# Attention's output divided in the layout of its sum and carried as rows by DMA to the gate's product

## The reference

```
src  = layernorm(x)
q, k, v = src @ q_w, src @ k_w, src @ v_w       # 16 heads of 16
s    = q k^T / 4 * (2 * sigmoid(sum(q * scale_w)))
out  = softmax(s) @ v                            # (2, 2048, 256)
gate = sigmoid(out @ gate_w + gate_b)
xr   = layernorm(src + (out * gate) @ out_w) * n1_g + n1_b
# router: top 2 of 8 experts from xr @ moe_gate_w, the one of larger index is applied,
# then two more layernorms and a residual
```

## Time and profile before

| | us |
|---|---|
| median of the runs | 2483.32 |
| the profiled execution | 2487.67 |
| its span, first to last instruction | 2487.7 |
| busy in the span: TensorE, VectorE, ScalarE, GpSimd | 2369.6, 2102.9, 1796.4, 992.7 |
| attention's units: first and last copy of `pv` to `pvs` start at | 822.5 and 2139.6 |
| first instructions of the gate's stage | 2143.5 |

### The profile page before, as it was taken

The page is one execution under the profiler, slowest core; times in us unless marked ns, Lnnn a source line. Parts: engine busy times, 40 slices in busy tenths (PEclk is TensorE's granted clock), DMA queues, the critical chain, the costliest instruction groups (busy, mean ns, idle before and its releaser), DMA issues. The chain is left out here.

```text
span 2487.7 us, 45337 instructions
## 1 busy us (share of the span) xinstructions
PE 2369.6 (95%) x16331; PEld 1028.3 (41%) x16331; DVE 2102.9 (85%) x4156; ACT 1796.4 (72%) x2368; POOL 992.7 (40%) x1186
## 2 busy tenths in 40 slices
PE   7899999999689999999999999999999999996996
PEld 5566655655443223223222222223223222473663
DVE  6778788989689999999998999898899996283886
ACT  4888887777334887878787787787787878762664
POOL 1687878888741222211221221221211011255664
PEclk8999999999889999999999999999999999997998
DMA  3322233223240220304012030040040000125892
GB/s 110 112 88 90 85 92 105 89 99 96 67 137 14 37 43 7 59 14 65 14 31 35 14 59 7 14 65 2 14 65 2 2 2 24 52 83 204 297 304 101
DMA packets 105956, 174.09 MB, mean 70 GB/s; under 512 B 21218, under 2 KB 80658, under 8 KB 100596
## 3 DMA queue, kind: packets, MB, share of 16 engines
q1 hardware_dynamic: 98996, 156.08, 23.6%
q0 software_dynamic: 6016, 14.49, 1.7%
q10 hardware_dynamic: 720, 0.62, 0.1%
HBM read 145.21 MB, written 27.02 MB: 69 GB/s over the span
## 5 line engine op out<-in xcount | busy, mean ns | idle before, releaser
L1682 DVE TENSOR_REDUCE max_part<-round_psum 128x1 f32<-128x512 f32 x2048 | 1269.0, 683 | 101.8 <-PE round_psum L1591 96.8
L1647 ACT ACTIVATE p_exp<-score_psum 128x1024 f32<-128x1024 f32 x1024 | 993.3, 1022 | 213.7 <-PE score_psum L1576 209.3
L1591 PE MATMUL round_psum<-k_stack,q_stack 64*128 64x512 bf16 x2048 | 705.5, 384 | 10.7 <-DVE max_part L1682 6.5
L1567 PE MATMUL score_psum<-q_stack,k_stack 64*128 64x512 bf16 x2048 | 599.0, 379 | 0.9 <-ACT p_exp L1647 0.2
L1576 PE MATMUL score_psum<-q_stack,k_stack 35*128 35x512 bf16 x2048 | 594.6, 378 | 0.0
L1622 PE MATMUL pv_psum<-p_exp,values 128*17 128x512 f32 x4096 | 539.6, 598 | 0.0
L1591 PEld LDWEIGHTS round_psum<-k_stack,q_stack 64*128 64x128 bf16 x2048 | 189.4, 93 | 600.3 <-DVE max_part L1682 510.7
L672 PE MATMUL rot<-tokens_t,w_in 128*128 128x512 f32 x576 | 271.7, 603 | 0.2
L1576 PEld LDWEIGHTS score_psum<-q_stack,k_stack 35*128 35x128 bf16 x2048 | 188.9, 94 | 116.0 <-issue 0.5
L1729 POOL TENSOR_TENSOR rden<-pv_out,minus_one 128x16 f32<-128x16 f32 x31 | 90.0, 2903 | 332.4 <-ACT pv_out L1665 330.1
L1715 POOL CAST max_parts<-max_neg 128x16 bf16<-128x16 f32 x96 | 20.4, 212 | 365.8 <-DVE max_neg L1688 343.4
(11 more groups left out here) (300 smaller groups left out, 3472.9 us busy)
## 6 DMA issues: line engine op xcount, KB each, us to landing
cum_rows_in<-cum_rows SPq DMA_DIRECT2D x64, 512.0 KB, 3.8
expert_w<-in_expert_w SPq DMA_DIRECT2D x24, 1028.0 KB
tokens_t<-in_expert_w SPq DMA_DIRECT2D x15, 1028.0 KB
cum_pairs_in<-cum_rows SPq DMA_DIRECT2D x240, 64.0 KB, 2.8
qk_rows<-qk_parts SPq DMA_DIRECT2D x64, 192.0 KB, 3.1
q_stack<-qk_rows SPq DMA_DIRECT2D x84, 128.0 KB, 8.1
k_stack<-qk_rows SPq DMA_DIRECT2D x84, 128.0 KB, 9.1
token_rows<-tokens SPq DMA_DIRECT2D x12, 512.0 KB, 3.7
```

Source lines behind the costliest of these rows:

```text
L1567: nc.tensor.matmul(ebank[i // 2][:, i % 2, :], ks[rows, n % 2, plane, k * P:(k + 1) * P], qs[rows, n % 2, plane, q * BLK:(q + 1) * BLK], s ...
L1591: nc.tensor.matmul(bank[step][:, :], qs[rows, n % 2, plane, at:at + P], ks[rows, n % 2, plane, keys * BLK:(keys + 1) * BLK], start=True, s ...
L1647: nc.scalar.activation(pt[:, (k * 2 + pair) % 4, :, :], ebank[pair][:, :, :], ACT.Exp).then_inc(*exped.up(u, k, pair))
L1682: nc.vector.tensor_reduce(mx[:, c * HG + h, keys:keys + 1], bank[step][:, :], AX_X, ALU.max).then_inc(*maxed.up(u, k, i))
```

## The change

`turn_out` and `turn` go. A unit's output stays in `pvs` with channels as rows and is divided there; that needs the denominators, one row per head, as inverses on each of the head's 16 rows. Five items, `OUT_AT`, take the place of `turn_out`: in step 2 of the next unit `out_low`: SP stores the four denominator rows to DRAM; step 3 `out_column`: SP loads them as a 128x16 tile; step 6 `out_inverse`: GpSimd's power, and SP stores the result; step 8 `out_spread`: SP loads each head's row of inverses to its 16 partitions (into `rspread`, the place of the value weights); step 11 `out_rows`: GpSimd multiplies 128x512, and SP copies each head's 16 rows by DMA to where `gate` reads them. ScalarE's next copy of `pv` waits for these copies instead of the division. The last unit spreads its denominators by four matmuls with a broadcast column of the identity, and VectorE takes the reciprocal and multiplies. `oT` is now a view of the tensor `tokens` itself, with the rows of all eight blocks. In the gate's stage `turn` is gone from the lists of TensorE and ScalarE, `xr` of a block is written over the block's rows in `oT`, and its store is two transfers. The lists and the `busy` counts are otherwise the same. The code behind SP's loop is unchanged.

```diff
+OUT_AT = (2, "out_low"), (3, "out_column"), (6, "out_inverse"), (8, "out_spread"), (11, "out_rows")
...
-        plan(u * KT + KT + 2, ("turn_out", u, 0, 0))
+        for wait, what in OUT_AT:
+            plan(u * KT + KT + wait, (what, u, 0, 0))
...
-    for t in range(-LEAD, total + 4):
+    for t in range(-LEAD, total + OUT_AT[-1][0] + 1):
...
+    rspread = S.w_v.rearrange("p k d -> p (k d)")
+    den_dram = nc.dram_tensor("denominators", (2, HG, BLK), F32, kind="Internal").ap()
+    inv_dram = nc.dram_tensor("denominator_inverses", (2, HG, BLK), F32, kind="Internal").ap()
+    oT = attn[:, :, :].rearrange("p c d -> p (c d)").rearrange("p (k t) -> p k t", k=KD)
...
-    users = [step for step in order if step[0] in ("max", "turn_rows", "turn_out", *splits)]
+    users = [step for step in order if step[0] in ("max", "turn_rows", *splits)]
...
+                if what == "out_low" and u < NU - 1:
+                    sp_.wait_ge(*pv_out.at(u))
+                    for h in range(HG):
+                        low = h * 32 + HD
+                        nc.sync.dma_start(den_dram[u % 2, h:h + 1, :],
+                                          pvs[low:low + 1, :]).then_inc(*den_saved.up(u, h))
+                if what == "out_column" and u < NU - 1:
+                    sp_.wait_ge(*den_saved.at(u, HG - 1))
+                    if u:
+                        sp_.wait_ge(*inv_saved.at(u - 1))
+                    nc.sync.dma_start(rden[:, :], den_dram[u % 2].rearrange("h (a w) -> (h a) w", w=CPB * HG)
+                                      ).then_inc(*den_load.up(u))
+                if what == "out_inverse" and u < NU - 1:
+                    sp_.wait_ge(*inverse.at(u))
+                    nc.sync.dma_start(inv_dram[u % 2].rearrange("h (a w) -> (h a) w", w=CPB * HG),
+                                      rden[:, :]).then_inc(*inv_saved.up(u))
+                if what == "out_spread" and u < NU - 1:
+                    sp_.wait_ge(*inv_saved.at(u))
+                    if u:
+                        sp_.wait_ge(*divided.at(u - 1))
+                    for h in range(HG):
+                        nc.sync.dma_start(rspread[h * 32:h * 32 + HD, :], inv_dram[u % 2, h:h + 1, :].to_broadcast([HD, BLK])
+                                          ).then_inc(*spread.up(u, h))
+                if what == "out_rows":
+                    n, q = UNITS[u]
+                    b, g = GROUPS[n]
+                    if u == 0:
+                        sp_.wait_ge(*x1_saved.all())
+                    sp_.wait_ge(*(divided if u < NU - 1 else last_divided).at(u))
+                    for h in range(HG):
+                        row = (g % 2) * HG * HD + h * HD
+                        nc.sync.dma_start(oT[row:row + HD, g // 2, b * SEQ + q * BLK:b * SEQ + (q + 1) * BLK],
+                                          pvs[h * 32:h * 32 + HD, :]).then_inc(*out_saved.up(u, h))
...
-                if what == "turn_out":
+                if what == "out_low" and u == NU - 1:
                     pe.wait_ge(*pv_out.at(u))
-                    pe.wait_ge(*bank_read(before[step]))
-                    for c in range(CPB):
-                        t = nc.tensor.transpose(bank[step][:, c * P:(c + 1) * P], pvs[:, c * P:(c + 1) * P], K["ident"])
-                    t.then_inc(*out_turned.up(u))
+                    pe.wait_ge(*exped.at(u, KT - 1, 1))
+                    for h in range(HG):
+                        low = h * 32 + HD
+                        m = nc.tensor.matmul(ebank[0][h * 32:(h + 1) * 32, 0, :], K["ident"][:, low:low + 1].to_broadcast([P, 32]),
+                                             pvs[:, :], start=True, stop=True, skip_group_check=True)
+                    m.then_inc(*last_spread.up(u))
...
                     if u:
-                        act.wait_ge(*divided.at(u - 1))
+                        act.wait_ge(*out_saved.at(u - 1, HG - 1))
                     nc.scalar.copy(pvs[:, :], pv[:, :]).then_inc(*pv_out.up(u))
-                if what == "turn_out" and u < NU - 1:
-                    act.wait_ge(*out_turned.at(u))
-                    nc.scalar.copy(pvs[:, :], bank[step][:, :]).then_inc(*out_in.up(u))
...
-                    nc.vector.reciprocal(rden[:, :].unsqueeze(2), o[:, :, HD:HD + 1]).then_inc(*last_inverse.up(u))
+                    nc.vector.reciprocal(rspread, ebank[0][:, 0, :]).then_inc(*last_inverse.up(u))
                     ve.wait_ge(*last_inverse.at(u))
...
+                    nc.vector.tensor_tensor(pvs[:, :], pvs[:, :], rspread, ALU.mult).then_inc(*last_divided.up(u))
...
+                if what == "out_inverse" and u < NU - 1:
+                    if u == 0:
                         po.wait_ge(*one.at(0))
+                    po.wait_ge(*den_load.at(u))
+                    nc.gpsimd.tensor_tensor(rden[:, :], rden[:, :], minus[:, :].to_broadcast([P, CPB * HG]),
+                                            ALU.pow).then_inc(*inverse.up(u))
+                if what == "out_rows" and u < NU - 1:
+                    po.wait_ge(*spread.at(u, HG - 1))
+                    nc.gpsimd.tensor_tensor(pvs[:, :], pvs[:, :], rspread, ALU.mult).then_inc(*divided.up(u))
...
-                        if c == 0:
-                            pe.wait_ge(*heads_t.at(b, k))
-                        m = nc.tensor.matmul(gbank[c][:, :], w_gate[:, k, c * P:(c + 1) * P], oT[:, two, k, :],
+                        if (b, c, k) == (0, 0, 0):
+                            pe.wait_ge(*G.out_saved.at(NU - 2, HG - 1))
+                        if (b, c, k) == (NBLK - 1, 0, 0):
+                            pe.wait_ge(*G.out_saved.at(NU - 1, HG - 1))
+                        m = nc.tensor.matmul(gbank[c][:, :], w_gate[:, k, c * P:(c + 1) * P],
+                                             oT[:, k, b * BLK:(b + 1) * BLK],
```

More of the change, by code:

```diff
@@ L1503, in attention @@
     v_stored = sems.events("late_v_stored", late)
[L1504 to L1505 removed]
+    den_saved = sems.dma("denominator_save", [(u, h) for u in range(NU - 1) for h in range(HG)])
+    den_load = sems.dma("denominator_load", range(NU - 1))
+    inverse = sems.events("denominator_inverse", range(NU - 1))
+    inv_saved = sems.dma("inverse_save", range(NU - 1))
+    spread = sems.dma("inverse_spread", [(u, h) for u in range(NU - 1) for h in range(HG)])
     divided = sems.events("out_divided", range(NU - 1))
+    out_saved = G.out_saved
+    last_spread = sems.events("last_denominator_spread", [NU - 1])
     last_inverse = sems.events("last_denominator_inverse", [NU - 1])
[L1508 removed]
+    last_divided = sems.events("last_out_divided", [NU - 1])
     one = sems.events("minus_one_ready", [0])
@@ L1689, in _ @@
                                             negate=True).then_inc(*negated.up(u))
-                if what == "turn_out" and u == NU - 1:
-                    n, q = UNITS[u]
-                    b, g = GROUPS[n]
-                    o = bank[step][:, :].rearrange("p (n w) -> p n w", w=32)
-                    ve.wait_ge(*out_turned.at(u))
+                if what == "out_inverse" and u == NU - 1:
+                    ve.wait_ge(*last_spread.at(u))
                     ve.wait_ge(*divided.at(u - 1))
-                    nc.vector.reciprocal(rden[:, :].unsqueeze(2), o[:, :, HD:HD + 1]).then_inc(*last_inverse.up(u))
+                    nc.vector.reciprocal(rspread, ebank[0][:, 0, :]).then_inc(*last_inverse.up(u))
                     ve.wait_ge(*last_inverse.at(u))
-                    for c in range(CPB):
-                        nc.vector.tensor_tensor(heads(attn[:, b * KT + q * CPB + c, g * HG * HD:(g + 1) * HG * HD],
-                                                          HG, HD), o[:, c * HG:(c + 1) * HG, 0:HD],
-                                                    over_last(rden[:, c * HG:(c + 1) * HG], HD), ALU.mult)
+                    nc.vector.tensor_tensor(pvs[:, :], pvs[:, :], rspread, ALU.mult).then_inc(*last_divided.up(u))
         @block.gpsimd
@@ L1794, in __init__ @@
         self.x1_load = [sems.dma(f"x1_load{i}", range(i, NBLK, 3)) for i in range(3)]
+        self.out_saved = sems.dma("out_save", [(u, h) for u in range(NU) for h in range(HG)])
 BIAS_AT = [slice(first, first + 3 * NE) for first in (0, 32)]
@@ L1826, in gate_and_route, with xr_block, by_two, over_block @@
     iota = {n: iotas[:, at] for n, at in I_AT.items()}
-    oT = sb("attn_t", [P, 2, KD, BLK])
+    oT = attn[:, :, :].rearrange("p c d -> p (c d)").rearrange("p (k t) -> p k t", k=KD)
+    def xr_block(b):
+        return oT[:, :, b * BLK:(b + 1) * BLK].rearrange("p k (two d) -> p k two d", d=D)
+    def by_two(t):
+        return t.rearrange("p (k two) d -> p k two d", two=2)
+    def over_block(row):
+        return row.unsqueeze(1).unsqueeze(1).to_broadcast([P, KD, 2, D])
     sig = sb("gate_sig", [P, 2, BLK])
@@ L1863, in gate_and_route @@
     halves = [(b, i) for b in range(NBLK) for i in range(2)]
-    t_users = [(what, b) for what, b in order["PE"] if what in ("turn", "rows")]
```

(28 more changed lines are left out.)

27 lines of the change are left out of this document (3 added, 24 removed), and 8 rows, old and new, of the table STAGE5.

## The result

The changed kernel takes 2492.76 us (median of nine runs, 2490.18 to 2498.70), the kernel before 2486.91 us (nine runs beside it). The ratio is 1.0030 (95% interval 1.0019 to 1.0041). A second set of twelve runs gave 1.0019 (1.0008 to 1.0030). So the change costs 0.2 to 0.3%, some 4 to 7 us, where a gain of 6.3 us was forecast.

The account below looks back on a forecast made before the run. VectorE was taken to set attention's pace, TensorE mattering where it makes VectorE wait. Terms -17.4 -1.0 +5.2 +8.5 +1.3 -0.9 -2.0 = -6.3 us, subtracted from the median, gave 2477.0 us, range 2468 to 2495.

Parts of the forecast that it names:

- 30 holes of 0.58 us, -17.4: Attention, VectorE: its 0.58 us wait after the four transposes of `turn_out` goes in 30 units, -17.4 us.
- unit 30, -1.0: Attention, unit 30: ScalarE no longer waits 0.43 us for transposes nor copies 0.58 us between exponentials, -1.0 us.
- (a): Attention: ScalarE's next `pv_out` waits for the row copies, one unit (40 us; 33 for the last) later: free.
- (b): Attention: SP carries the maxima's rows (`turn_rows`, step 13) behind `out_rows` (step 11): free by 6 us or more.
- (c): Attention: GpSimd has `out_rows` ahead of `negate`; free in quiet units, 1.3 us in each of four `low` units, +5.2 us.
- the sign: Attention, SP: an issue of `turn_rows` that waited for anything but its rows would show the forecast wrong.
- The chain of transfers: Attention: from `pv_out`'s copy through saves, loads, power and spreads to the product, 19.2 us, 26 beside stack transfers; cost 0.
- the 30.5: Attention: GpSimd's product must end by about 30.5 us after the end of `pv_out`'s copy to cost nothing.
- the rival of an overrun in seven units: Attention, seven stack units: two transfer hops wait, the product ends at 33 us, 17.5 us lost, 2495 us; chance 0.17.
- The boundary, +8.5 and +1.3: Last copy to the gate's first matmul grows from 7.5 to 16.0 us, +8.5; TensorE's slow clock on gate matmuls, +1.3.
- Stage 5, -2.0: Behind the gate's start: without `turn3` and `turn4` VectorE waits 1.2 us less for `norm1`, plus 0.8 of smaller waits, -2.0 us.
- The experts, nothing: Last scatter to the end: forecast change 0.

Follow-up runs that it names:

- Two candidates: Kernel before with one part added at a time: each block's row store split in two, ratio 0.9998; two small DRAM tensors made and written once, ratio 1.0001.

## Why the prediction was wrong

The measured 2492.8 us lies inside the stated 2468 to 2495, but by luck: the upper end stood for another way of being slower, which did not happen. (Of its chances, 0.53 x 0.25 + 0.10 is 0.23 and not 0.24.) By the prediction's own steps:

- **30 holes of 0.58 us, -17.4, and unit 30, -1.0: right.** With the four bad units mended attention is 19.8 us shorter, 1.4 more than these two; no run shows where the 1.4 come from.
- **(a) ScalarE's next copy waits for nothing: right** in the changed kernel. It is no law: three steps later it is wrong (the run with the store in step 14).
- **(b) "SP carries the maxima's rows behind `out_rows`: free by 6 us or more": this step failed.** It holds in the other units. In the four with `low` in step 11 the product comes late, and the prediction itself had said so under (c); it priced there what GpSimd's lateness does to TensorE and did not carry it on to SP, which waits for the same product. That product ends 31.9 us after the saves begin, not 19.2. Behind that wait stand four row copies (2.46 us), `save` (2.54 us) and the maxima's rows (2.90 us). Cost: 11.5 us of holes in the first profile, 9.8 in the second, 11.9 in the third. The prediction had named the sign itself: an issue of `turn_rows` on SP that waits for anything but its rows. The run with only SP's part moved shows that SP's queue is the cause of these holes, as they went while GpSimd's order stayed.
- **(c) GpSimd's parts late by the product's 1.3 us, +5.2: right in kind, too large.** The hole grew by 0.57 us in each of four, 2.3 us. So the term for the `low` units was +5.2 and measured 14.1 with both: 1311.4 us (mean of three) against 1297.3 with `out_rows` in step 10.
- **The chain of transfers: free, as forecast, but by two errors that offset each other.** 19.2 us from the copy to the product's end were estimated, and 7 more in the stack units, 26. In the quiet unit at 1861 the saves start at 1861.34 and the product ends at 1874.1: 12.8 us. In the stack unit at 1296.61 it ends at 1321.2: 24.6 us, 11.8 more. One hop makes 8.2 of them, the inverses' save, whose landing SP awaits before it issues the spreads: 9.65 us, and 1.46 in the quiet unit.

```profile
1307.01 0.34 SPq L1567 DMA_DIRECT2D denominator_inverses<-rden  x1
...
1316.66 1.70 SPq L1574 DMA_DIRECT2D w_v<-denominator_inverses  x4
```

  Five of the seven stack units end 22.7 to 25.9 us after the saves begin; in the first two the product stands behind split work on GpSimd and ends at 31.0 and 33.9, past the 30.5, and no hole of VectorE is longer there than in the kernel before. So the rival of an overrun in seven units, the prediction's slower case, did not happen; the kernel is slower by another road.
- **The boundary, +8.5 and +1.3: right as a sum, in part by luck.** The transfers were cheaper: row copies 2.4 us (2.8), loads 4.2 (5.35, of which the last one's 1.68 became 0.39); the barrier was 2.0 (1.7). The clock was dearer: 12.62, 11.97 and 12.54 us for 24 matmuls in the three profiles against 10.46 at the full rate, 2.2, 1.5 and 2.1 us (1.3). The reciprocal took 3.36 us and was put at 3.3, but through a slip: 0.1 us lies between 4 and 16 columns, which is 12 columns and not 16. So 512 columns would add 4.2 us and make some 4.4, and the row of 4 columns is of another operation. By the Trainium skill's eight repeats ("VectorE: DVE Perf Modes", section "First, the fixed hardware budget") an estimated 4.3 or more; the trace does not bear that out.
- **Stage 5, -2.0: wrong, +0.6.** VectorE's wait for `norm1` did shrink, from 2.26 to 1.38 us; two writes of 1.23 us became 2.32 and 2.18. Once the two no longer meet, the stage is 97.4 us, 1.5 less than the mean before. The prediction asked what TensorE and ScalarE do with the removed turns and not which of GpSimd's products would then meet VectorE.
- **The experts, nothing: +4.4 us between the means of three and four profiles.** That part stays open. Two candidates showed nothing when put in one at a time; what is left (the different moment at which the stage begins, the state of the DMA queues) was not tried.

The misses add up to 7.6 (attention), -0.4 (boundary), 2.6 (stage 5), 4.4 (experts, cause open) and 0.1 us ahead of attention, 14.3 us between the forecast of -6.3 and the +8.0 between the mean spans of these profiles. The timed runs say +4 to +7. Of attention's 7.6 the four units make 8.9 (14.1 less the 5.2 forecast), and the removals gave 1.4 more than forecast.

## What to carry to other kernels

When an item is put into an order that all engines share, go through it once for each engine that has a part in it: its place behind a wait on one engine becomes a wait on every other one, and the queue behind that is where the price is paid. Where one unit in eight has something else in the same step, look at that unit; one step earlier was worth 13 us. Work at a stage's end that only the next stage's last block needs belongs behind the barrier, where an engine idles anyway: here that was worth 9.5 us, more than the 6.5 of the issues and the arithmetic moved, in part because TensorE's clock no longer fell (1.5 us of the gate's matmuls, 0.4 of the fillers).

## What the runs showed of the hardware that was not expected

- Four stores of one row of 2 KB each from SBUF to DRAM took SP 1.10 us to issue, 0.28 us each; four copies of 16 rows between places in SBUF 2.40 to 2.46 us in the rows shown, 2.90 and 3.38 beside stack transfers.
- A reciprocal of 128x512 from PSUM takes VectorE 3.36 us, five times a product of the same size (0.69 us).
- TensorE stood 2.5 us at the boundary without a fall of its rate afterwards. After stops of 0.69 and 2.67 us with 0.66 us of work between them the granted clock was 0.50 for some 3.4 us. After 12.9 us the fillers and the first matmuls were slow (granted clock 0.50; 12.62 us for 24, 10.46 at the full rate).
- A save of 8 KB to DRAM, issued behind some 20 stack transfers of 128 KB, kept SP waiting 9.65 us for its landing; alone it took 1.46 us.
- VectorE and GpSimd, both with operands in SBUF, hold each other up by 0.5 to 1.1 us when they meet.
